# A graph block on one core: edges ahead in the MLP stage, five scatter tables, an early edge batch, 16-bit destinations

## What is computed

```python
xn = layernorm(x)
summed = segment_sum(edge_attr_64, dst, 6250)          # the edges' features, by destination
count = segment_sum(ones, dst, 6250)
agg = summed / max(count, 1)
gnn = xn + relu(concat([xn, agg]) @ W1 + b1) @ W2 + b2  # 576 -> 1024 -> 512
mix = flow_attention(xn)                                # q, k, v of 8 heads, sigmoids, softmax over nodes
x = x + gnn + mix
xn2 = layernorm(x)
e = argmax(softmax(mean(xn2, nodes) @ Wg + bg))         # one of 16 experts for all nodes
x = x + gate[e] * (xn2 @ We[e] + be[e])
```

## Time and profile before

| | us |
|---|---|
| three runs, median (lowest to highest) | 2417.53 (2413.97 to 2419.3) |
| the profiled execution, its own time | 2420.85 |
| its span, first to last instruction | 2419.1 |
| PE busy in the span | 1961.3 (81%) |
| POOL busy, of which the scatters | 1377.2 (57%), 1302.1 |
| DVE busy | 1226.5 (51%) |
| ACT busy | 556.6 (23%) |
| mean granted PE clock | 0.864 of full speed |

### The profile page before, as it was taken

The page is one execution under the profiler, slowest core; times in us unless marked ns, Lnnn a source line. Parts: engine busy times, 40 slices in busy tenths (PEclk is TensorE's granted clock), DMA queues, the critical chain, the costliest instruction groups (busy, mean ns, idle before and its releaser), DMA issues. The chain is left out here.

```text
span 2419.1 us, 32814 instructions
## 1 busy us (share of the span) xinstructions
PE 1961.3 (81%) x10775; PEld 1548.8 (64%) x10775; DVE 1226.5 (51%) x3857; ACT 556.6 (23%) x1317; POOL 1377.2 (57%) x948
## 2 busy tenths in 40 slices
PE   2999999999999989974578776677619888888498
PEld 1787878788787874442467665566417667766386
DVE  4444444443444416664466644545347667665375
ACT  2322222223322211112112211111013233222210
POOL 0878888888878886667576767777811111111100
PEclk9999999999999996567588876667859898989699
DMA  8778787887877779879889999888554554542594
GB/s 288 159 158 168 156 179 153 173 163 153 171 161 157 152 154 250 227 190 227 173 170 201 207 170 174 159 166 149 71 170 153 174 167 140 177 149 74 199 310 164
DMA packets 510484, 420.69 MB, mean 174 GB/s; under 512 B 342747, under 2 KB 379627, under 8 KB 510334
## 3 DMA queue, kind: packets, MB, share of 16 engines
q1 hardware_dynamic: 382542, 364.17, 51.7%
q0 software_dynamic: 127792, 54.60, 23.1%
HBM read 267.57 MB, written 151.08 MB: 173 GB/s over the span
## 5 line engine op out<-in xcount | busy, mean ns | idle before, releaser
L269 POOL DMA_INDIRECT table<-edge_sums,edge_row x831 | 1302.1, 1567 | 457.6 <-issue 261.6
L216 DVE SCALAR_TENSOR_TENSOR edge_sel<-edge_dst_all,edge_dst_f,upper 128x128 f32<-128x128 int32 x831 | 328.7, 452 | 100.4 <-PE edge_sum L228 100.2
L228 PE MATMUL edge_sum<-edge_attr,edge_sel 128*128 128x65 f32 x1662 | 250.8, 300 | 140.2 <-DVE edge_sel L216 138.8
L228 PEld LDWEIGHTS edge_sum<-edge_attr,edge_sel 128*128 128x128 f32 x1662 | 235.8, 214 | 192.8 <-DVE edge_sel L216 167.7
L326 PE MATMUL pr_out_bank<-pr_norm_xT_hi,pr_w_hi 128*128 128x512 f32 (+1 forms) x832 | 329.5, 396 | 0.0
L326 PE MATMUL pr_out_bank<-pr_norm_xT_lo,pr_w_hi 128*128 128x512 f32 (+1 forms) x832 | 320.8, 386 | 0.0
L326 PE MATMUL pr_out_bank<-pr_norm_xT_hi,pr_w_lo 128*128 128x512 f32 (+1 forms) x832 | 320.5, 385 | 0.0
L238 ACT ACTIVATE edge_sums<-edge_sum 128x260 f32<-128x260 f32 (+1 forms) x209 | 80.8, 387 | 717.7 <-PE edge_sum L228 607.2
L326 PE MATMUL gn_acc<-gn_w_hi,gn_h_hi 128*128 128x512 f32 (+1 forms) x392 | 164.5, 420 | 21.3 <-DVE gn_h_lo L1861 21.3
L326 PEld LDWEIGHTS pr_out_bank<-pr_norm_xT_lo,pr_w_hi 128*128 128x128 f32 x832 | 156.6, 188 | 34.0
L326 PEld LDWEIGHTS pr_out_bank<-pr_norm_xT_hi,pr_w_lo 128*128 128x128 f32 x832 | 157.1, 189 | 30.0
(11 more groups left out here) (198 smaller groups left out, 3302.2 us busy)
## 6 DMA issues: line engine op xcount, KB each, us to landing
edge_dst_all<-in_dst SPq DMA_DIRECT2D x103, 512.0 KB, 5.5
edge_attr<-in_edge_attr SPq DMA_DIRECT2D x103, 256.0 KB, 6.0
qk_T<-pr_stage SPq DMA_DIRECT2D x48, 512.0 KB, 3.2
h_pre_T<-pr_stage SPq DMA_DIRECT2D x48, 512.0 KB, 3.4
gn_pre<-h_pre_T SPq DMA_DIRECT2D x12, 2048.0 KB, 12.1
done<-qk_T SPq DMA_DIRECT2D x16, 1024.0 KB, 5.8
table<-edge_sums,edge_row POOLq DMA_INDIRECT x831
pr_norm_x<-in_x SPq DMA_DIRECT2D x12, 1024.0 KB, 8.6
```

Of the source, the lines that this page charges most:

```text
L216: op = dve.scalar_tensor_tensor(out=self.sel[q][0:rows, j, 0:rows], in0=self.dst_all[k][0:rows, t:t + m * (rows - 1) + 1:m], scalar=self.d ...
L228: mm = pe.matmul(self.p_sum[q][0:rows, j * ECOLS:(j + 1) * ECOLS], self.sel[q][0:rows, j, 0:rows], self.attr[k][0:rows, j0 + j, :], start= ...
L269: pool.indirect_dma_start(self.c.table[t], bass.IndirectOffsetOnAxis(ap=self.row[k][0:rows, j:j + 1], axis=0), self.sums[k][0:rows, j, :], ...
```

## The change

1. **Tables.** Five scatter tables instead of four. Tiles take them in turn over all batches (tile number mod 5), not anew in each batch. POOL's program is written out whole. Five tables of zeros are written instead of four, and the MLP stage loads and adds up five.
2. **Start.** In the constants stage the destinations are loaded, converted to 16 bits on DVE and written to a new tensor `dst16`; `dst_all` is loaded from it (256 KB a batch). Batch 0 is loaded right after x of block 0 and selected, summed and kept before the first block is worked. Then come the zero tables, then the two DMAs of `w_qkv`, three batches, the bias, the two DMAs of `w1`, then x of block 1. Weights are loaded and split in four pieces instead of eight.
3. **Shares.** One batch early, then 57, 9, 4 and 34. Attention's block 11 takes the last one (10 edges), block 10 and those before it three each.
4. **MLP stage.** Tables are loaded and added up three blocks ahead, at the block's end on DVE; `agg` has three buffers. PE turns the sums of block b+2 after subtile 1, and ACT and DVE split them there. ACT's copy of subtile 3's transpose moves behind the next block's first square root and hidden parts, and DVE's `add_part` of it to subtile 1. The hidden parts are spread 3, 3, 2 over the subtiles instead of 2, 3, 3.
5. `sem_inc(c.passed, 1)` goes from the scatter and the MLP stage.

The core of the diff:

```diff
-TABLES = 4
+TABLES = 5
+EARLY = 1
-SHARE_A = [5, 4, 5, 4, 5, 4, 5, 4, 5, 4, 5, 5, 1]
-SHARE_B = [1, 0, 1, 1, 0, 1, 1, 0, 1, 1, 0, 1, 0]
-SHARE_C = [1, 0, 0, 1, 0, 0, 1, 0, 0, 1, 0, 1, 0]
-SHARE_D = [3, 3, 3, 3, 3, 3, 3, 3, 3, 3, 3, 3, 0]
+SHARE_A = [5, 4, 5, 4, 5, 5, 4, 5, 5, 4, 5, 5, 1]
+SHARE_B = [1, 1, 1, 0, 1, 1, 1, 0, 1, 1, 1, 0, 0]
+SHARE_C = [1, 0, 0, 1, 0, 0, 1, 0, 0, 1, 0, 0, 0]
+SHARE_D = [3, 3, 3, 3, 3, 3, 3, 3, 3, 3, 3, 1, 0]
...
-        self.dst_all = sb("dst_all", [P, BATCH * P], I32)
+        self.dst_all = sb("dst_all", [P, BATCH * P], I16)
...
-            t = j % TABLES
+            tile = g * BATCH + j if g <= WHOLE else WHOLE * BATCH + LEFT[0][0] + j
+            t = tile % TABLES
...
-            pool.wait_ge(self.c.scattered[t], g * (16 * BATCH // TABLES) + 16 * (j // TABLES))
-            pool.sem_inc(self.c.passed, 1)
+            if tile >= TABLES:
+                pool.wait_ge(self.c.scattered[t], tile // TABLES * 16)
...
-        with pool.Fori(0, looped) as i:
-            for k in range(SLOTS):
-                self.scatter(pool, i * SLOTS + k, k)
-        for g in range(looped * SLOTS, NBATCH):
+        for g in range(NBATCH):
             self.scatter(pool, g, g % SLOTS)
...
+            sp.dma_start(dst_i[:, 0:EACH], c.dst[0:P * EACH].rearrange("(p m) -> p m", p=P)).then_inc(biases_in, 16)
...
+            sp.wait_ge(converted, 2)
+            sp.dma_start(c.dst16[0:P * EACH].rearrange("(p m) -> p m", p=P), dst_h[:, 0:EACH]).then_inc(biases_in, 16)
...
+            sp.wait_ge(biases_in, 80)
...
+            dve.tensor_copy(dst_h[:, 0:EACH], dst_i[:, 0:EACH]).then_inc(converted, 1)
...
-        weights.load(sp)
         edges.begin_sp(sp)
-        for g in range(LEAD):
-            edges.load(sp, g, g)
-        sp.dma_start(bias_v[:, :], c.b_v.partition_broadcast(P)).then_inc(bias_v_in, 16)
+        edges.load(sp, 0, 0)
         sp.wait_ge(zero_set, 1)
         for t in range(TABLES):
             sp.dma_start(c.table[t].rearrange("(p b a) c -> p b (a c)", p=P, b=5),
...
+        weights.load(sp, 0, 2)
+        for g in range(1, EARLY + LEAD):
+            edges.load(sp, g, g % SLOTS)
+        sp.dma_start(bias_v[:, :], c.b_v.partition_broadcast(P)).then_inc(bias_v_in, 16)
+        weights.load(sp, 2, 4)
         norm.load(sp, 1, 1, BT)
...
+        for g in range(EARLY):
+            for q in range(2):
+                edges.select(dve, g, g, q)
+                edges.rows(dve, g, g, q)
         norm.first_on_dve(dve)
...
-        SLOTS_OF = ((0, 1), (2, 3, 4), (5, 6, 7))
+        SLOTS_OF = ((0, 1, 2), (3, 4, 5), (6, 7))
+        AGGS = 3
...
             def body(b, k, n, after):
+                if later_size(b, 3):
+                    sp.wait_ge(agg_step, b * 4 + 9)
+                    load_tables(b + 3, later_size(b, 3))
                 if later_size(b, 2):
-                    sp.wait_ge(agg_step, b * 4 + 8)
-                    sp.sem_inc(c.passed, 1)
-                    load_tables(b + 2, later_size(b, 2))
                     sp.wait_ge(hid_ready, b * JH + (JH + AHEAD))
...
                     if 1 <= s < ns:
                         turned(b, n, s - 1)
-                if later_size(b, 2):
-                    agg_high(b + 2, k, later_size(b, 2))
-                turned(b, n, ns - 1)
+                    if s == 0 and b:
+                        turned(b - 1, BT, CH - 1)
+                    if s == 1 and later_size(b, 2):
+                        agg_high(b + 2, k, later_size(b, 2))
+                if not after:
+                    turned(b, n, ns - 1)
...
-                    if ahead and s == 0:
-                        add_tables(b + 2, ahead)
-                    if ahead and s == 1:
-                        divide_sums(b + 2, ahead)
...
                 if ahead:
-                    split_agg(b + 2, k, ahead)
+                    add_tables(b + 3, ahead)
+                    divide_sums(b + 3, ahead)
```

More of the change, by code:

```diff
@@ L276, in finish_pool @@
         for t in range(TABLES):
-            count = sum(len([j for j in range(shape_of(g)[0]) if j % TABLES == t]) for g in range(NBATCH))
-            pool.wait_ge(self.c.scattered[t], 16 * count)
+            pool.wait_ge(self.c.scattered[t], 16 * len(range(t, WHOLE * BATCH + sum(m for m, rows in LEFT), TABLES)))
     def scatter_all(self, pool):
-        looped = WHOLE // SLOTS
-        with pool.Fori(0, looped) as i:
-            for k in range(SLOTS):
-                self.scatter(pool, i * SLOTS + k, k)
-        for g in range(looped * SLOTS, NBATCH):
+        for g in range(NBATCH):
             self.scatter(pool, g, g % SLOTS)
@@ L299, in __init__, with load @@
         self.sems = self.loaded + [self.hi_ready, self.lo_ready]
-    def load(self, sp):
-        for (src, raw, hi, lo), loaded in zip(self.items, self.loaded):
+    def load(self, sp, first=0, last=None):
+        for (src, raw, hi, lo), loaded in list(zip(self.items, self.loaded))[first:last]:
             sp.dma_start(raw, src).then_inc(loaded, 16)
@@ L555, in project_stage @@
         weights = Weights(c.front, nc, "pr_w", [
-            (c.w_qkv[i * P:(i + 1) * P, :], stage[:, i * W3:(i + 1) * W3], w_hi[:, i, :], w_lo[:, i, :])
-            for i in range(CH)] + [
-            (c.w1[i * P:(i + 1) * P, :], norm.early[:, i * HID:(i + 1) * HID],
-             w1_hi[:, i, :], w1_lo[:, i, :]) for i in range(CH)])
+            (c.w_qkv[i * P:(i + 2) * P, :].rearrange("(o p) f -> p o f", p=P),
+             stage[:, i * W3:(i + 2) * W3].rearrange("p (o f) -> p o f", o=2), w_hi[:, i:i + 2, :], w_lo[:, i:i + 2, :])
+            for i in (0, 2)] + [
+            (c.w1[i * P:(i + 2) * P, :].rearrange("(o p) f -> p o f", p=P),
+             norm.early[:, i * HID:(i + 2) * HID].rearrange("p (o f) -> p o f", o=2), w1_hi[:, i:i + 2, :],
+             w1_lo[:, i:i + 2, :]) for i in (0, 2)])
         v_mm, v_bank_free, v_stored = sem("v_mm"), sem("v_bank_free"), sem("v_stored")
@@ L621, in pe_program @@
         pe.sem_inc(out_mm, 1)
+        for g in range(EARLY):
+            for q in range(2):
+                edges.sum_tile(pe, g, g, q)
         for s in range(CH):
             norm.turn(pe, 0, BT, s, s - 1 if s >= 2 else None)
-        weights.wait(pe, CH)
+        weights.wait(pe, 2)
         def body(b, k, n, after):
@@ L639, in body @@
                     if e == QK:
-                        weights.wait(pe, 2 * CH)
+                        weights.wait(pe, 4)
                     pe.wait_ge(out_free, b * OUTS + e + 1)
@@ L652, in act_program @@
     def act_program(act):
+        edges.begin_act(act)
+        for g in range(EARLY):
+            for q in range(2):
+                edges.keep(act, g, g, q)
         norm.deviation(act, 0, BT)
@@ L689, in dve_program @@
     def dve_program(dve):
+        edges.begin_dve(dve)
         dve.memset(zero[:, :], 0.0).then_inc(zero_set, 1)
-        edges.begin_dve(dve)
+        for g in range(EARLY):
+            for q in range(2):
+                edges.select(dve, g, g, q)
+                edges.rows(dve, g, g, q)
         norm.first_on_dve(dve)
@@ L1618, in gnn_stage @@
         agg_inv = sb("agg_inv", [P, CH])
-        agg = [sb(f"agg{k}", [P, BT], F32R) for k in range(2)]
+        agg = [sb(f"agg{k}", [P, BT], F32R) for k in range(AGGS)]
         pre = [sb(f"pre{k}", [P, JH, BT]) for k in range(2)]
```

67 lines of the change are left out of this document (37 added, 30 removed).

## The result

Four runs of the changed kernel give a median of 2347.49 us (2344.9 to 2349.22), four of the kernel before on the same chip 2418.41 us (2413.97 to 2422.58). The ratio is 0.9722 (95% interval 0.9695 to 0.9749): 71 us faster. The prediction said 2322 with a range of 2272 to 2376: 99 us were forecast (from the profiled execution, 2420.85) and 71 came. The profiled execution took 2349.22 us, its span is 2347.5, and the mean granted clock rose from 0.864 to 0.889.

A forecast was written before the change was run, and what follows sets the result against it. The prediction took POOL's scatters, held by waits for their tables, to bound the front from 1387 us on. From the profiled 2420.85 us, -65 (front) and -34 (MLP stage) gave 2322 us, range 2272 to 2376.

The forecast's parts named there:

- The front: Everything ahead of the MLP stage: to end at 1708.5 us against 1773.2, -65 us.
- Start and projection: Start +9.5 us from later loads, projection +2.2 us from one more batch.
- Norms: Norms stage: one more batch costs DVE selects and small steps, +4.5 us.
- Scale: Scale stage: one batch less, -3 us (bounds 0 and -6.7).
- Attention: Attention stage: five tables give 1.90 us per scatter and 43 us per block, ten blocks 430 us instead of 478.
- The 16 bits: Attention: the 16-bit broadcast of destinations saves 2.6 us of DMA per block.
- The rival that DMA keeps attention: Attention: saved bytes worth nothing, five tables wait as four do, 46.5 us per block, +35, 2357 us; chance 0.20.
- POOL's written-out program: POOL's scatter loop written out: 0 us (bounds -15 and +20); by the skill's page 15 us would come back, 2307.
- part 3: MLP stage: reordering saves 3.5 us per block, -35 over ten blocks; with the fifth table's costs -34 us.
- the stores bound the MLP stage: Rival, MLP stage: POOL's store landings take what ACT's new order gives, no gain there, 2356 us; chance 0.15.
- The MLP stage at PE's pace: Rival: MLP blocks take 28 to 30 us near full clock, another -50, 2272 us; chance 0.12.
- dropped counts: MLP stage: removing unread counts after waits gives 0 us, at the far end -19.

The follow-up runs named there:

- tables_only: `unrolled` plus a fifth scatter table, tables taken in turn over all tiles, nothing else: 2361.8 us.
- four_tables: The changed kernel with four scatter tables instead of five, all else as changed: 2372.6 us.
- wide_dst: The changed kernel with the destinations broadcast in 32 bits again instead of 16: 2354.7 us.
- mlp_only: The kernel before with the changed kernel's MLP stage programs, still four tables: 2408.74 us.
- stores_free: The changed kernel with a semaphore per x1 and transpose buffer in the MLP stage, so POOL waits for no store there: 2275.06 us, ratio to the kernel before 0.9425.
- free_before: The kernel before with only the buffer semaphores of `stores_free` added, so POOL waits for no MLP-stage store: 2334.27 us, ratio 0.9662.
- free_old_order: `front_only` with the buffer semaphores of `stores_free`, so POOL waits for no MLP-stage store: 2278.61 us, ratio to the kernel before 0.9433.
- written_only: The kernel before with POOL's scatter program written out and all counts kept: 2412.81 us, ratio 1.0.
- front_only: The changed kernel with the MLP stage programs of the kernel before, with five tables: 2346.05 us.
- unrolled: The kernel before with POOL's scatter program written out and all seventeen lines of unread counts removed, four tables and old shares: 2398.23 us.
- unrolled_again: The same kernel as `unrolled`, timed again in rounds: 2398.44 us, ratio to the kernel before 0.9938.
- zeros_last: The changed kernel with the zeros of the five tables written behind all other loads of the start: 2355.67 us, ratio to the kernel before 0.9758.

## Why the prediction was right, and where not

**The bound of the front was read rightly.** POOL's wait for its tables kept it back; five tables took 76 us of waits to 12.3, and `tables_only` and `four_tables` show that it was the table. The front was forecast at -65. It came at -70.3 in the two profiles, and at -65.7 between the means of all profiles with the old front and with the new. By its terms:

- Start and projection: +11.7 forecast, +13 measured (the last output at 907 against 894). POOL began at 44.02 where 41 stood, the second batch came at 73.63 and not 70, PE's first edge sum behind the early batch at 70.50 and not 68.
- Norms +4.5: 4 measured, by the first instructions of the stages (the windows above are cut more coarsely). Scale -3: -7, the far bound. The first base store moved by 5.3 us in the two profiles, by 9.4 between the means, and not 13.
- Attention: 430 us for ten blocks forecast, 437.1 measured (426.1 to 437.1 in the four profiles, 432 in the mean). A scatter was to take 1.90; POOL did 203 from 1300 to 1694.5, 1.94 each. Blocks 11 and 12 and the barrier took 42.2 us where 47.5 stood (46.8 in the mean). The distance of base stores was to be 42 to 45 to the end; the last two are 49.1 and 46.8.
- The 16 bits were to spare 2.6 us of DMA in each attention block. `wide_dst` shows at most 1 us of it in each of the first five blocks and none over all ten (43.4 against 43.7). The first five go at DMA's pace, 41.7 us where 41.5 stood, while POOL falls behind; later the slots are full and POOL sets the distance. The bytes count at the start instead, 4 us, and 7.6 by the projection's end. The rival that DMA keeps attention (46.5 us per block, waits for tables as before) falls: its busy share of 0.99 was that of a stretch in which the slots were being filled, and is no bound of the later one.
- POOL's written-out program: 0 forecast, ratio 1.0 measured. The Trainium skill (Runtime: NRT & Kernel Launch, Instruction fetch mechanics) states a stall for a taken branch whose target isn't in the two pages of instructions held by the engine. No cost of it is to be seen here: the loop's run and the written-out one are the same within 0.24%. Whether this loop's branch meets the page's condition no row shows, so the run speaks against the 15 us that the prediction names beside its 0, and not against the page.

**The step that failed is part 3, -34 us for the MLP stage.** It came out at -1.8 (485.0 to 483.2; -6.0 in `mlp_only`, which has one table less; base loads 35.0 us apart, where 31 to 34 stood), and the rival "the stores bound the MLP stage" (2356, given 0.15) describes what happened. The time still lies in the range because the range was drawn around that rival too, and because the front, which is the larger part, came as forecast. The argument had both facts and weighed them wrongly. It priced the wait of DVE for the square root as time that comes back, and gave 1.5 us per block for POOL's buffers. But a wait at a consumer is no price. The rows beside it, POOL's 135.7 + 125.5 us of waits for landings and 49 times two stores of 0.55 and 0.76 us, can be summed. In the kernel after that sum is 404.9 of 428.6 us. In the one before the whole trace has 125.5 us and

```profile
POOL x_rows L1952 <- DMA x1n_T<-gn_x1nT: 138.9, 34, 7.4
...
POOL x1n_T L1960 <- DMA x1n_T<-gn_x1nT: 40.5, 12, 3.7
...
POOL x_rows L1952 <- DMA x_rows<-gn_x: 24.8, 10, 2.5
```

With the stores' 64.2 that is 393.9 of the 426.6 from 1822.9 to 2249.5: a chain 92% full. Whatever is reordered beside such a chain moves waits from one engine to another and leaves the period, 35.8 and 35.0 us. `stores_free` and `free_before` show it directly: the chain gone, the period is 28.3 us in the new order and 29.0 in the old (29.6 in `free_old_order`). "The MLP stage at PE's pace" was a rival with 2272 us, on the condition that stores never hold DVE. With that condition supplied the time is 2275.

The **dropped counts** were taken at 0 with a far end of -19 for the MLP stage, because the gap of the earlier trace rows is 0.30 us with a count in it and without. All counts of the kernel before together cost 14.4 us. So a count that the gap of one instruction doesn't show can still cost. The single profiles put it on both sides: the MLP stage in the old order takes 485.0, 481.5 and 486.1 us with counts (before, `written_only`, `front_only`) and 474.3, 477.2 and 472.7 without (`unrolled`, `unrolled_again`, `tables_only`), 9.5 less in the mean. The new order, without counts, takes 483.2, 482.9, 479.3, 479.0 and 479.0 (changed kernel, `wide_dst`, `zeros_last`, `four_tables`, `mlp_only`), 481 in the mean. Against a full chain the new order thus looks 6 us worse than the old, and the dropped counts hide it. This rests on one profile of each kernel and wasn't tested by itself; a plausible cause is that the copy of subtile 3 stands ahead of the next x1 in POOL's queue, as the prediction noted.

Part of what the free stores give comes with the clock: over the whole MLP stage it was 0.88 and 0.89 in the changed kernel, and is 0.94 in each of the three kernels with free stores. From 1773 to 2050 us a product of the second layer (`gn_acc<-gn_w_hi,gn_h_hi`) took a mean of 418 ns in the changed kernel and 395 in `stores_free`. How much of this is the clock stays open, for in `free_before` it took 402 ns there at a granted clock of 0.93, next to the 0.94 of the changed kernel.

The best version of this study is `stores_free`: 2275.06 us, faster than both kernels.

## What to carry to other kernels

When an engine issues a store, waits for it to land and then issues the next, add up its stores and its waits over the stage. Where the sum is near the stage's time, that chain is the bound, however little the engine is "busy" (POOL 13% here), and the waits seen at other engines can be its echoes, as the square root's was here, and no gain to be had. Give each buffer a semaphore and let the engine that writes the buffer wait for it, and price a reorder only after that. Where one engine has no slack in a stage (POOL in the projection here), look first at when it can start: `zeros_last` gave the others a start 23 us sooner and POOL one 22 us later, and came out no faster.

## What the runs showed of the hardware

- POOL's `x_rows` store of 256 KB lands a median 2.3 us after its issue, the transpose's 3.5 us. With issue and queueing, two stores in series took 8.7 us (428.6 / 49). The Trainium skill (DMA: Bandwidth & Descriptors, Anatomy of one DMA — SWDGE (gpsimd) path) gives a fixed cost of about 2.0 us per DMA, mostly the receipt of the write. The 2.3 us of x1 are near it, the transpose's 3.5 are not, and with free stores the medians are 4.9 and 4.5. An estimate from that page: 98 stores in series take at least 98 x 2.0 = 196 us whatever they carry.
- Scatters with nothing to wait for keep 1.86 us each over 400 us at a stretch (215 of them in each of the three windows shown).
- Semaphore increments behind waits, though nothing reads them, cost 0.6% of the kernel (ratio 0.9938 without them, 1.0 with them, both with POOL's program written out).
- PE without a gap from 1773 to 2050 us (`stores_free`) was granted a clock of 1.00; with gaps of 31 us (the changed kernel) 0.94 in the same stretch, with gaps of 28 (`free_before`) 0.93, but with gaps of 9 (`free_old_order`) 1.00. So gaps in PE's work can cost twice here, once as idle time and once in the products between them, and not every gap does.
